# Adding the causal mask of the row maxima on VectorE inside the maximum, and making the last stage's weight parts on GpSimd alone

## The chip, the cores and the metric

The kernel runs on one core of a Trainium2 chip. The metric is the device time of one execution in microseconds (us), the median of the runs. TensorE is called PE below, VectorE DVE, ScalarE ACT, GpSimd Pool, and SP is the engine whose queue issues most DMAs. The engines run in parallel and meet only through semaphores.

## The reference, cut to what matters

Four layers follow one another on x of shape (2, 1024, 512): attention a, a feed-forward layer, attention b, the same feed-forward layer again, each behind a layer norm and with its input added. The change touches attention b, which is causal and has a linear bias per head, and the preparation of the weights of the stage behind it:

```
H, D = 32, 16
scores = jnp.einsum('bqhd,bkhd->bhqk', q, k) * SCALE
causal = rel <= 0
scores = jnp.where(causal[None, None], scores + bias[None], -jnp.inf)
attn = jax.nn.softmax(scores, axis=-1)
out = jnp.einsum('bhqk,bkhd->bqhd', attn, v).reshape(B, S, HIDDEN)
return out @ w_proj + b_proj
```

Everything is fp32. The kernel splits some operands into a high part with fewer mantissa bits and the low part that is left, and multiplies the parts.

## The kernel before, in words

The program is a chain of stages: the projections of attention a (tag pa), attention a (tag a), the stage that applies a's output projection, the feed-forward layer and b's projections (tag mid), attention b (tag b), and the last stage with b's output projection and the feed-forward layer (tag fin). Both attentions are built by one function, `attention`, and `causal` is true for b only.

**Tiling of attention.** A group is four heads of one batch element; there are 16 groups, and one step of the loop handles one group. The keys of a group lie along the free axis in row tiles: two heads (`e` = 0 and 1) sit in partitions 0 to 63 and 64 to 127 of the same tensor, so that their products use two different halves of PE's rows. A step computes each group's scores twice. The first time is for the **maxima**: a *piece* is the product of 128 queries with up to 512 keys of one head, into one of three PSUM banks (`ps_m`, `MXB = 3`), and DVE reduces it to one maximum per query (`reduce_piece`, L513). In attention b a group has 48 pieces; pieces on the diagonal are cut to 128, 256, 384 or 512 keys, and 32 of the 48 pieces are diagonal, 8 of each width. The second time is for the **scores** with keys in the partitions (`scores`, L417, into `ps_s`), where the negated maximum enters as extra rows of the product; ACT takes the exponential (L492, into `p_sb`), and `values` (L436) multiplies by the values into `ps_o`. ACT copies `ps_o` out twice a step (`copy_out`, L483), the second time at the end of the step.

**The mask.** On the diagonal the pieces and the scores both need -1e30 where the key lies after the query. `add_mask` (L355) puts it into PSUM ahead of the product: two bf16 products of a mask (64 rows by 128 columns as weights) with a half identity, 64 columns each; the product of the piece then adds to it. So each diagonal piece takes three products, and so does each diagonal score product. `mask_of_query` serves the pieces, `mask_of_key` the scores. One DMA (L333) loads the masks at the start of attention b; PE waits for it before the first piece.

**The order of the work.** PE's order is written out by hand. The pieces run 13 units ahead of the scores (`AHEAD`), which is one unit more than the 12 units of a step: the loop of step s does the scores, exponentials and values of group s and the maxima of group s + 1. Between two score products come the pieces of `ahead`. Step 15, the last, has no maxima beside it. Ahead of step 0 the first 52 pieces run with filler products between them (`keep_clock`). PE waits in `maxima` for `piece_taken` (a bank comes free), in `scores` for `exp_done` of the tile before the last, in `values` for both exponentials of the unit. DVE waits for `piece_ready`. Once a half of a group has all its maxima, DVE negates them (L519), Pool makes a high and a low part of them (`parts_of_maxima`, L266 and L269), PE turns them, DVE copies them out, and SP writes them beside the queries.

**The weights of the last stage.** `w_proj` and `w_eff` (128 x 2048 each) are needed in two parts by stage fin. Pool issues the load of `w_proj` in its loop at g = 2. ACT makes the high parts behind step 13 (`s == NG - 3`, L504), two copies in a row in ACT's own queue, ahead of the exponentials of step 14. Pool makes the low parts (L284) behind its last `parts_of_maxima`, those of group 15, and has nothing else queued until the stage ends.

Of the kernel before, what the change touches and what calls it, by code (L numbers as in the profile page):

```python
# [7 lines left out]
ALU = mybir.AluOpType  # L8
# [6 lines left out]
P = 128  # L15
# [124 lines left out]
def attention(nc, tag, causal, scale, consts, q_d, k_d, v_d, o_d, z_d, alibi_d, ones_d, first, more, output, late, to_split):  # L140
# [56 lines left out]
    with ExitStack() as ctx:  # L197
        def sb(name, shape, dt):
            return ctx.enter_context(nc.sbuf_tensor(f"{tag}_{name}", shape, dt))
# [12 lines left out]
        cparts = sb("cparts", [P, PAIR, SHIFT_ROWS, ROWS_H // PAIR], F32R)  # L212
        cturned = sb("cturned", [TURNED, P], F32)
        if causal:
            masks = sb("masks", [P, 2 * 2 * P + ROW_TILE], BF16)
            mask_of_query = masks[:, 0:2 * P].rearrange("p (a n) -> p a n", a=2)
            mask_of_key = masks[:, 2 * P:4 * P].rearrange("p (a n) -> p a n", a=2)
            half_ident = masks[:, 4 * P:]
        ps_s = ctx.enter_context(nc.psum_tensor(f"{tag}_ps_s", [P, 4, CHUNK], F32))
        ps_m = ctx.enter_context(nc.psum_tensor(f"{tag}_ps_m", [P, MXB, CHUNK], F32))  # L220
        ps_o = ctx.enter_context(nc.psum_tensor(f"{tag}_ps_o", [P, CHUNK], F32))
# [27 lines left out]
        @block.gpsimd  # L249
        def _(pool):  # L250

            pool.memset(zeros[:, :], 0.0).then_inc(zeroed, 1)
            pool.wait_ge(zeroed, 1)
            slots[1].load_k(pool, k_d, 1, alibi_d, first_loaded[0])

            def split(columns):
                return columns.rearrange("p (e n) -> p e n", e=PAIR)

            def parts_of_maxima(g, qh):

                pool.wait_ge(negated, g * 2 + (qh + 1))

                if (g, qh) != (0, 0):
                    before = turned_item(g, 0) if qh else turned_item(g - 1, 1)
                    pool.wait_ge(piece_taken, before + 1)
                pool.tensor_tensor(cparts[:, :, 0, :], split(negm[:, :]), split(zeros[:, :]),  # L266
                                   ALU.subtract).then_inc(high_ready, 1)
                pool.wait_ge(high_ready, g * 2 + (qh + 1))
                pool.tensor_tensor(cparts[:, :, 1, :], split(negm[:, :]), cparts[:, :, 0, :].bitcast(F32),  # L269
                                   ALU.subtract).then_inc(parts_ready, 1)  # L270

            parts_of_maxima(0, 0)
            slots[2].load_k(pool, k_d, 2, alibi_d, first_loaded[1])
            parts_of_maxima(0, 1)
            for g in range(1, NG):
                for qh in range(2):
                    parts_of_maxima(g, qh)
                if g == 2:
                    for to, source in late:
                        pool.dma_start(to, source).then_inc(late_loaded, 16)  # L280
            pool.wait_ge(late_loaded, 16 * len(late))
            for n, (whole, high, low_part) in enumerate(to_split):
                pool.wait_ge(w_high_ready, n + 1)
                pool.tensor_tensor(low_part[:, :, :], whole[:, :, :], high[:, :, :].bitcast(F32),  # L284
                                   ALU.subtract).then_inc(w_split, 1)
            if to_split:
                pool.wait_ge(w_split, len(to_split))
# [57 lines left out]
        def _(pe):  # L345
# [12 lines left out]
            def maxima(g, j, i):  # L358

                pair, e, qt, half, keys = pieces[i]  # L360
                if i == 0:

                    if causal and g == 0:
                        pe.wait_ge(masks_loaded, 16)
                    if j:
                        pe.wait_ge(rows_set, SETS)
                        pe.wait_ge(first_loaded[j - 1], K_LOAD)
                    wait_past(pe, qk_loaded[j], loads(g) * LOAD - (K_LOAD if j else 0))

                wait_past(pe, piece_taken, item(g, i) + (1 - MXB))  # L370
                row = ROW_TILE * e
                q = slots[j].q[row:row + crow, qt // 4, pair, qt % 4 * P:(qt % 4 + 1) * P]
                k = slots[j].k[row:row + crow, pair, half * CHUNK:half * CHUNK + keys]
                diagonal = causal and half == qt // 4
                if diagonal:
                    add_mask(ps_m[:, bank_of(g, i), keys - P:keys], mask_of_query, row)
                pe.matmul(ps_m[:, bank_of(g, i), 0:keys], q, k, start=not diagonal, stop=True,  # L377
                          skip_group_check=diagonal).then_inc(piece_ready, 1)

            def turn_maxima(g, qh):  # L380

# [95 lines left out]
        @block.scalar  # L477
        def _(act):
            def copy_out(s, qh):

                act.wait_ge(pv_done, s * NU + (last_of[qh] + 1))
                wait_past(act, out_stored[qh], s * output.STORES)
                act.activation(o_sb[:, qh, :], ps_o[:, :], ACT.Copy).then_inc(out_copied, 1)  # L483

            def step(s):
                for u, (qh, kt) in enumerate(units):
                    off = max(0, P * kt - CHUNK * qh) if causal else 0

                    wait_past(act, pv_done, s * NU + (u - 1))
                    for pair in range(2):  # L490
                        act.wait_ge(score_ready, s * NT + (2 * u + pair + 1))
                        act.activation(p_sb[:, (2 * u + pair) % NP, :, off:CHUNK],  # L492
                                       ps_s[:, 2 * pair:2 * pair + 2, off:CHUNK], ACT.Exp,
                                       scale=scale).then_inc(exp_done, 1)
                    if u == last_of[0] + 1:
                        copy_out(s, 0)
                copy_out(s, 1)

            for s in range(NG):
                step(s)  # L500
                if s == NG - 3 and to_split:
                    act.wait_ge(late_loaded, 16 * len(late))
                    for whole, high, _ in to_split:
                        act.activation(high[:, :, :], whole[:, :, :], ACT.Copy).then_inc(w_high_ready, 1)  # L504

        @block.vector
        def _(dve):
            def reduce_piece(g, i):
                pair, e, qt, half, keys = pieces[i]
                at = e * (ROWS_H // PAIR) + pair * 4 + qt % 4  # L510
                to, from_ = mxp[:, qt // 4, at, half:half + 1], ps_m[:, bank_of(g, i), 0:keys]
                dve.wait_ge(piece_ready, item(g, i) + 1)
                dve.tensor_reduce(to, from_, AX.X, ALU.max).then_inc(piece_taken, 1)  # L513

            def negated_maxima(g, qh):

                dve.wait_ge(piece_taken, item(g, (NPH, NPC)[qh] - 1) + 1)
                wait_past(dve, parts_ready, g * 2 + qh)
                dve.tensor_reduce(negm[:, :], mxp[:, qh, :, :], AX.X, ALU.max, negate=True).then_inc(negated, 1)  # L519

            def copy_turned(g, qh):
                dve.wait_ge(piece_ready, turned_item(g, qh) + 1)

                wait_past(dve, shift_loaded, g * (2 * SHIFT) + SHIFT * qh)
                dve.tensor_copy(cturned[:, :], ps_m[0:TURNED, turned_bank(g, qh), 0:P]).then_inc(piece_taken, 1)

            def ahead(s, lo, hi):

                for x in range(lo, hi):
                    past, i = divmod(x, NPC)  # L530
                    g = s + past
                    if g < NG:
                        reduce_piece(g, i)
                    if i == PPU - 1 and 0 < g <= NG:
                        copy_turned(g - 1, 1)
                    if g < NG:
                        if i == NPH + PPU - 1:
                            copy_turned(g, 0)
                        if i + 1 in (NPH, NPC):
                            negated_maxima(g, int(i + 1 == NPC))  # L540

            dve.memset(mxp[:, :, :, :], LOWEST).then_inc(filled, 1)
            dve.wait_ge(filled, 1)
            ahead(0, 0, AHEAD)
            for s in range(NG):
                ahead(s, AHEAD, AHEAD + NPC)
                if s == NG - 2:
                    output.reciprocals(dve, 0)
            output.scale(dve, 0)
# [992 lines left out]
def shape_constants():  # L1542
# [8 lines left out]
        else:  # L1551
            rot[i - DH // 2, i] = 1.0
    row, column = (np.arange(P) % ROW_TILE)[:, None], np.arange(P)[None, :]
    masks = [np.where(row + half * ROW_TILE > column, NEG, 0.0) for half in range(2)]
    masks += [np.where(column > row + half * ROW_TILE, NEG, 0.0) for half in range(2)]
    masks = np.concatenate(masks + [np.where(row == np.arange(ROW_TILE)[None, :], 1.0, 0.0)], axis=1)
    base = 2 ** (-2 ** (-(np.log2(H) - 3)))
    slopes = (base ** np.arange(1, H + 1, dtype=np.float32)).astype(np.float32)

# [35 lines left out]
```

## Time and profile before

| what | value |
|---|---|
| median of 3 runs | 1870.08 us (1851.12, 1870.08, 2012.93) |
| profiled execution, its own time | 1866.97 us |
| its span, first to last instruction | 1865.1 us, 0.2% under the median of the runs |
| mean granted TensorE clock | 0.949 of 2.4 GHz |
| PE busy over the span | 1744.0 us, 94% |
| DVE busy over the span | 1366.6 us, 73% |
| ACT busy over the span | 987.7 us, 53% |
| Pool busy over the span | 119.7 us, 6% |
| attention b, first piece to the last copy of the output | from about 1186 to 1735 us |
| last stage (fin), from that copy to the end | 130.5 us |

Times in the profile count from the start of the span. A group of instructions is given with its busy time and the mean of one in ns. Matmuls are pipelined: the busy time of one reaches from its start to the arrival of its last result, and two that run beside each other overlap, so the rate of PE is read from the distance between starts and not from busy times. The granted clock is 1.00 at 2.4 GHz and 0.50 at 1.2 GHz. "Idle before" is the time for which the engine did nothing ahead of an instruction, and the name behind the arrow is what ended it.

### The profile page before, as it was taken

How to read it: one execution, taken by the hardware profiler on the slowest of the kernel's cores; microseconds unless marked ns; L12 is line 12 of the kernel's file. 1: busy time of each engine (PE TensorE's matmuls, PEld its weight loads, DVE VectorE, ACT ScalarE, POOL GpSimd, SP SyncE). 2: the span in 40 equal slices, each digit the busy share in tenths (PEclk: the TensorE clock that was granted, in tenths of full speed). 3: DMA queues.
4: the chain of work that ended last, by engine and by line, in shares of the span. 5: the costliest groups of instructions: out<-in, count | busy, mean ns of one | idle time of the engine just before them, and what ended most of it. 6: DMA issues, size and time to landing. Idle time of an engine off the chain costs nothing. (4 is left out here: it accounts for less than half of the span.)

```text
span 1865.1 us, 35240 instructions
## 1 busy us (share of the span) xinstructions
PE 1744.0 (94%) x14412; PEld 904.9 (49%) x14412; DVE 1366.6 (73%) x2495; ACT 987.7 (53%) x1169; POOL 119.7 (6%) x218
## 2 busy tenths in 40 slices
PE   6997999999999999999799998899999999999697
PEld 4553433333333333333347677555555555543486
DVE  3765799999999999996464542588787878762485
ACT  3332277777777777778301111056666666655210
POOL 3323000000000000000010000100000000002000
PEclk9998799999999999999899999999999999975699
DMA  7768304332333333321524246815445444511221
GB/s 212 211 190 213 63 15 87 65 70 53 53 53 56 53 53 53 64 46 58 149 64 135 69 115 208 160 28 107 81 80 89 72 84 77 87 30 56 83 85 68
DMA packets 116865, 167.67 MB, mean 90 GB/s; under 512 B 20828, under 2 KB 58092, under 8 KB 116588
## 3 DMA queue, kind: packets, MB, share of 16 engines
q1 hardware_dynamic: 114880, 160.11, 38.1%
q0 software_dynamic: 1824, 5.31, 1.6%
q8 instruction: 114, 1.87, 0.4%
q14 instruction: 47, 0.39, 0.1%
HBM read 100.34 MB, written 64.50 MB: 88 GB/s over the span
## 5 line engine op out<-in xcount | busy, mean ns | idle before, releaser
L513 DVE TENSOR_REDUCE a_mxp<-a_ps_m 128x1 f32<-128x512 f32 x1024 | 634.2, 683 | 48.3 <-PE a_ps_m L377 44.9
L492 ACT ACTIVATE a_p<-a_ps_s 128x1024 f32<-128x1024 f32 x512 | 522.4, 1025 | 170.6 <-PE a_ps_s L417 160.9
L513 DVE TENSOR_REDUCE b_mxp<-b_ps_m 128x1 f32<-128x512 f32 (+3 forms) x768 | 382.3, 551 | 116.8 <-PE b_ps_m L377 109.6
L492 ACT ACTIVATE b_p<-b_ps_s 128x1024 f32<-128x1024 f32 (+3 forms) x384 | 308.8, 810 | 231.3 <-PE b_ps_s L417 229.0
L377 PE MATMUL a_ps_m<-a_slot_qk 48*128 48x512 f32 x640 | 240.0, 452 | 0.9
L417 PE MATMUL a_ps_s<-a_slot_qk 50*128 50x512 f32 x640 | 233.1, 445 | 1.2
L436 PE MATMUL a_ps_o<-a_p,a_slot_v 128*32 128x256 f32 x2560 | 205.6, 390 | 10.0 <-ACT a_p L492 5.4
L417 PEld LDWEIGHTS a_ps_s<-a_slot_qk 50*128 50x128 f32 x640 | 96.4, 185 | 128.8 <-issue 122.7
L377 PE MATMUL a_ps_m<-slot_qk 48*128 48x512 f32 x384 | 145.7, 469 | 0.4
L417 PE MATMUL a_ps_s<-slot_qk 50*128 50x512 f32 x384 | 140.3, 466 | 2.2 <-DMA slot_qk<-a_cturned 1.6
L436 PE MATMUL a_ps_o<-a_p,slot_memory 128*32 128x256 f32 x1536 | 127.9, 403 | 7.3 <-ACT a_p L492 3.3
L355 PE MATMUL b_ps_m<-b_masks 64*128 64x64 bf16 x1024 | 116.5, 197 | 2.3 <-DVE b_mxp L513 2.3
L436 PEld LDWEIGHTS a_ps_o<-a_p,a_slot_v 128*32 128x32 f32 x2560 | 54.9, 108 | 115.2 <-ACT a_p L492 101.7
L377 PE MATMUL b_ps_m<-o_qk 50*128 50x512 f32 (+3 forms) x288 | 106.3, 446 | 0.4
L355 PE MATMUL b_ps_s<-b_masks 64*128 64x64 bf16 x1024 | 102.8, 201 | 3.1 <-ACT b_p L492 3.1
L377 PEld LDWEIGHTS a_ps_m<-a_slot_qk 48*128 48x128 f32 x640 | 99.4, 185 | 9.2 <-DVE a_mxp L513 8.0
L417 PEld LDWEIGHTS a_ps_s<-slot_qk 50*128 50x128 f32 x384 | 57.6, 192 | 83.0 <-issue 76.0
L634 PE MATMUL mid_ps<-mid_q_xnt,mid_w_qkv 128*128 128x512 f32 x384 | 90.9, 398 | 5.6 <-DVE mid_q_xnt L1408 5.6
L355 PEld LDWEIGHTS b_ps_s<-b_masks 64*128 64x128 bf16 x1024 | 51.3, 97 | 90.6 <-issue 66.0
L417 PE MATMUL b_ps_s<-o_qk 52*128 52x512 f32 (+3 forms) x288 | 94.7, 453 | 0.2 <-ACT b_p L492 0.2
L417 PE MATMUL b_ps_s<-b_slot_qk 52*128 52x512 f32 (+3 forms) x240 | 86.9, 453 | 0.0
L377 PE MATMUL b_ps_m<-b_slot_qk 50*128 50x512 f32 (+2 forms) x240 | 85.8, 413 | 0.5
(166 smaller groups left out, 2453.7 us busy)
## 6 DMA issues: line engine op xcount, KB each, us to landing
va_groups<-w_o SPq DMA_DIRECT2D x16, 512.0 KB, 3.7
ka_parts<-pa_parts SPq DMA_DIRECT2D x16, 512.0 KB, 3.8
qa_parts<-pa_parts SPq DMA_DIRECT2D x32, 256.0 KB, 3.7
kb_parts<-slot_memory SPq DMA_DIRECT2D x16, 512.0 KB, 3.5
qb_parts<-slot_memory SPq DMA_DIRECT2D x32, 256.0 KB, 3.5
vb_groups<-w_proj SPq DMA_DIRECT2D x16, 512.0 KB, 3.2
a_slot_qk<-qa_parts SPq DMA_DIRECT2D x60, 128.0 KB, 4.5
a_slot_qk<-ka_parts SPq DMA_DIRECT2D x48, 128.0 KB, 6.9
```

The costliest lines, as they stand in the source:

```text
L355: pe.matmul(to[:, half * ROW_TILE:(half + 1) * ROW_TILE], mask[tile, half, :], half_ident[tile, :], start=(half == 0), stop=False, skip_gr ...
L377: pe.matmul(ps_m[:, bank_of(g, i), 0:keys], q, k, start=not diagonal, stop=True, skip_group_check=diagonal).then_inc(piece_ready, 1)
L417: mm = pe.matmul(ps_s[:, PAIR * pair + e, off:CHUNK], k, q, start=not diagonal, stop=True, skip_group_check=diagonal)
L436: mm = pe.matmul(ps_o[VW * h:VW * (h + 1), lo:hi], slots[j].v[:, kt, VW * h:VW * (h + 1)], p_sb[:, (2 * u + h // 2) % NP, h % 2, lo:hi], s ...
L492: act.activation(p_sb[:, (2 * u + pair) % NP, :, off:CHUNK], ps_s[:, 2 * pair:2 * pair + 2, off:CHUNK], ACT.Exp, scale=scale).then_inc(exp ...
L513: dve.tensor_reduce(to, from_, AX.X, ALU.max).then_inc(piece_taken, 1)
L634: mm = pe.matmul(out, lhs[a](kc), rhs[b](kc), start=(n == 0), stop=(n == len(steps) - 1))
```

## The change

The mask of the maxima is no longer put into PSUM by PE. PE issues only the product of the piece. DVE adds a mask to a diagonal piece and takes the maximum in one instruction, `tensor_tensor_reduce`: it reads the piece from PSUM and a bf16 mask from SBUF, writes the sum back into the same PSUM bank, and writes the running maximum to `mxp`. The mask for DVE is 512 columns wide, zeros and then the triangle, of which the last `keys` columns are taken; the loaded tensor grows from 576 to 832 columns. The masks of the scores stay as they are. DVE waits once for the masks' load, in group 0. The other 16 pieces of a group keep `tensor_reduce`.

The high parts of `w_proj` and `w_eff` are made by Pool, each ahead of its low part, in Pool's queue behind the last `parts_of_maxima`; the two copies on ACT are gone.

```diff
-                diagonal = causal and half == qt // 4
-                if diagonal:
-                    add_mask(ps_m[:, bank_of(g, i), keys - P:keys], mask_of_query, row)
-                pe.matmul(ps_m[:, bank_of(g, i), 0:keys], q, k, start=not diagonal, stop=True,
-                          skip_group_check=diagonal).then_inc(piece_ready, 1)
+                pe.matmul(ps_m[:, bank_of(g, i), 0:keys], q, k, start=True, stop=True).then_inc(piece_ready, 1)
...
-                dve.tensor_reduce(to, from_, AX.X, ALU.max).then_inc(piece_taken, 1)
+                if causal and half == qt // 4:
+                    if g == 0:
+                        dve.wait_ge(masks_loaded, 16)
+                    dve.tensor_tensor_reduce(from_, from_, mask_of_query[:, CHUNK - keys:], 1.0, LOWEST,
+                                             ALU.add, ALU.max, accum_out=to).then_inc(piece_taken, 1)
+                else:
+                    dve.tensor_reduce(to, from_, AX.X, ALU.max).then_inc(piece_taken, 1)
...
             for n, (whole, high, low_part) in enumerate(to_split):
+                pool.tensor_copy(high[:, :, :], whole[:, :, :]).then_inc(w_high_ready, 1)
                 pool.wait_ge(w_high_ready, n + 1)
...
-                if s == NG - 3 and to_split:
-                    act.wait_ge(late_loaded, 16 * len(late))
-                    for whole, high, _ in to_split:
-                        act.activation(high[:, :, :], whole[:, :, :], ACT.Copy).then_inc(w_high_ready, 1)
```

## Rows read from the trace of the kernel before

**Rows 1.** The page, part 2: PE busy and granted clock in 40 slices of the span.
```profile
PE   6997999999999999999799998899999999999697
...
PEclk9998799999999999999899999999999999975699
```

**Rows 2.** Busy time by stretch: steps 1 to 13, step 14, step 15, the last stage.
```profile
core 0: us, PE busy (x) PEld busy (x) DVE busy (x) ACT busy (x) POOL busy (x), PEclk, DMA share, GB/s
1247.36:1648.05 400.69, 397.17 (x5050) 214.60 (x5046) 319.74 (x676) 263.65 (x339) 12.09 (x53) 1.00 0.48 84
1648.05:1698.82 50.77, 48.13 (x382) 23.37 (x378) 26.31 (x50) 23.86 (x29) 6.15 (x6) 0.55 0.04 10
1698.82:1734.62 35.80, 34.25 (x272) 12.42 (x268) 2.50 (x4) 20.11 (x26) 3.69 (x1) 0.50 0.25 72
1734.62:1865.10 130.48, 104.71 (x448) 84.98 (x448) 87.14 (x162) 17.96 (x33) 4.06 (x4) 0.88 0.25 84
```

**Rows 3.** Timeline of ACT around the end of step 13: start, us, engine, line.
```profile
1648.05 0.60 ACT L483 ACTIVATE out_b_sums<-b_ps_o 128x512 f32<-128x512 f32 x1 [0.63 <-PE b_ps_o L436]
1648.54 1.90 ACT L504 ACTIVATE w_proj_high<-w_proj 128x2048 fp32r<-128x2048 f32 x1
1650.34 1.90 ACT L504 ACTIVATE w_eff_high<-w_eff 128x2048 fp32r<-128x2048 f32 x1
1652.14 1.93 ACT L492 ACTIVATE b_p<-b_ps_s 128x1024 f32<-128x1024 f32 x2
```

**Rows 4.** Timeline of PE behind them.
```profile
1653.21 0.23 PE L355 MATMUL b_ps_s<-b_masks 64*128 64x64 bf16 x1 [2.64 <-ACT b_p L492]
```

**Rows 5.** Busy time in short stretches on either side of a change of the clock.
```profile
1195.50:1198.90 3.40, 3.08 (x18) 1.45 (x17) 2.46 (x6) 0.00 (x0) 3.24 (x8) 1.00 1.07 154
205.70:209.10 3.40, 1.83 (x8) 0.88 (x8) 2.19 (x4) 0.00 (x0) 0.00 (x0) 1.00 0.46 58
209.10:212.50 3.40, 3.40 (x16) 1.91 (x18) 3.03 (x6) 2.21 (x3) 0.00 (x0) 0.50 0.00 0
...
1649.50:1652.90 3.40, 1.07 (x13) 0.75 (x12) 1.63 (x5) 3.40 (x3) 0.00 (x0) 1.00 0.22 48
1652.90:1656.30 3.40, 3.09 (x32) 1.76 (x32) 0.89 (x3) 1.98 (x3) 0.00 (x0) 0.51 0.15 41
```

**Rows 6.** Timeline of PE in step 7: a diagonal piece with its two masks.
```profile
1443.14 0.23 PE L355 MATMUL b_ps_m<-b_masks 64*128 64x64 bf16 x2
1443.21 0.36 PE L377 MATMUL b_ps_m<-b_slot_qk 50*128 50x256 f32 x1
```

**Rows 7.** Waits between 1220 and 1640: us in total, times, longest.
```profile
DVE b_mxp L513 <- PE b_ps_m L377: 76.6, 137, 1.4
...
PEld b_ps_m L355 <- DVE b_mxp L513: 14.2, 43, 0.5
...
PEld b_ps_m L377 <- DVE b_mxp L513: 7.6, 28, 0.3
```

**Rows 8.** Groups of DVE's instructions by shape, between 1220 and 1640: busy us, mean ns.
```profile
L513 DVE TENSOR_REDUCE b_mxp<-b_ps_m 128x1 f32<-128x512 f32 x330 | 209.6, 683 | 33.2 <-PE b_ps_m L377 31.9
...
L513 DVE TENSOR_REDUCE b_mxp<-b_ps_m 128x1 f32<-128x128 f32 x108 | 26.0, 281 | 2.3 <-PE b_ps_m L377 2.3
```

**Rows 9.** Groups of DVE over the whole span: other forms that take two tensors, and a small one.
```profile
L1391 DVE SCALAR_TENSOR_TENSOR slot_memory<-mid_ps,b_qk,slot_memory 128x512 fp32r<-128x512 f32 x32 | 23.5, 749 | 45.7 <-ACT slot_memory L1331 45.7
...
L1379 DVE TENSOR_TENSOR x_sb<-mid_ps,x_sb 128x512 f32<-128x512 f32 x32 | 21.1, 686 | 36.4 <-PE mid_ps L1284 36.4
...
L519 DVE TENSOR_REDUCE b_negm<-b_mxp 128x16 f32<-128x32 f32 x32 | 5.9, 186 | 1.1
```

**Rows 10.** Timeline of Pool in steps 14 and 15.
```profile
1693.32 0.22 POOL L269 TENSOR_TENSOR b_cparts<-b_negm,b_cparts 128x16 fp32r<-128x16 f32 x1
1693.50 4.52 POOL L284 TENSOR_TENSOR w_proj_low<-w_proj,w_proj_high 128x2048 fp32r<-128x2048 f32 x1
1697.97 4.54 POOL L284 TENSOR_TENSOR w_eff_low<-w_eff,w_eff_high 128x2048 fp32r<-128x2048 f32 x1
```

**Rows 11.** Group of Pool: the nearest row to a plain write of 128 x 2048.
```profile
L983 POOL MEMSET w_o<- 128x2048 f32 x1 | 1.8, 1804 | 0.3 <-POOLq L1584 0.3
```

More of the change, by code:

```diff
@@ L214, in attention @@
         if causal:
[L215 to L218, printed above, removed]
+            masks = sb("masks", [P, 2 * P + ROW_TILE + CHUNK], BF16)
+            mask_of_key = masks[:, 0:2 * P].rearrange("p (a n) -> p a n", a=2)
+            half_ident = masks[:, 2 * P:2 * P + ROW_TILE]
+            mask_of_query = masks[:, 2 * P + ROW_TILE:]
         ps_s = ctx.enter_context(nc.psum_tensor(f"{tag}_ps_s", [P, 4, CHUNK], F32))
@@ L1553, in shape_constants @@
     row, column = (np.arange(P) % ROW_TILE)[:, None], np.arange(P)[None, :]
-    masks = [np.where(row + half * ROW_TILE > column, NEG, 0.0) for half in range(2)]
-    masks += [np.where(column > row + half * ROW_TILE, NEG, 0.0) for half in range(2)]
-    masks = np.concatenate(masks + [np.where(row == np.arange(ROW_TILE)[None, :], 1.0, 0.0)], axis=1)
+    masks = [np.where(column > row + half * ROW_TILE, NEG, 0.0) for half in range(2)]
+    masks += [np.where(row == np.arange(ROW_TILE)[None, :], 1.0, 0.0), np.zeros((P, CHUNK - P))]
+    masks += [np.where(column > np.arange(P)[:, None], NEG, 0.0)]
+    masks = np.concatenate(masks, axis=1)
     base = 2 ** (-2 ** (-(np.log2(H) - 3)))
```

## The prediction

> **What bounds the kernel now.** I read the page first, for the clock by slices [rows 1]: PE is busy nearly everywhere, and its clock falls under 0.9 in few slices, most of all in the three from about 1632 us on, which are the end of attention b and the start of the last stage. Then I cut attention b by steps, from one end-of-step copy on ACT to the next [rows 2]. Steps 1 to 13 take 400.69 us, 30.82 us each, all at clock 1.00. PE is busy for 99% of them by the page's way of counting, DVE for 24.6 us a step (319.74 / 13, 80%), ACT for 20.3 us (66%). Step 14 has the same work, takes 50.77 us, and its clock is 0.55. Step 15, without maxima, takes 35.80 us at 0.50.
>
> The reason for step 14 stands in the timelines. At the end of step 13 ACT makes the two high parts, from 1648.54 to 1652.24, before the first exponential of step 14 [rows 3]; PE runs out of free score banks and idles for 2.64 us until 1653.21 [rows 4]. In the short stretch around this gap PE is busy for 1.07 of 3.40 us, and behind it the clock is 0.5, that is 1.2 instead of 2.4 GHz [rows 5]. The same had happened at 209 us: 1.83 busy of 3.40, and the next stretch is at 0.50. With 3.08 of 3.40 the clock stayed at 1.00 [rows 5]. It stays low to the end of attention b: 48.13 us of step 14 without the gap against 30.82.
>
> **Part 1, the copies leave ACT.** Step 14 loses the gap and keeps the clock: 50.77 - 30.82 = 19.95 us saved. Step 15 at the full clock is on no row. Scaled as step 14 is (30.82 / 48.13 = 0.64) it takes 22.9 us; ACT alone is busy for 20.1 of it [rows 2] and becomes a larger share, so I take 24 us, a saving of 11.8. The bounds are 20.1 (ACT without a pause, 15.7 saved) and 35.8 (the clock is lost again before it, nothing saved). The last stage behind it is left at its 130.48 us; it begins with a chain of stores and loads while PE idles, so its clock starts low either way.
>
> **Part 2, Pool takes them.** Pool's queue is empty behind the last parts of the maxima. There the two low parts run now, 4.52 and 4.54 us [rows 10]. No row shows a Pool copy of 128 x 2048: the bounds are a fill, 1.80 us [rows 11], and the subtraction that reads two inputs, 4.52. With 4.5 (it reads and writes, nearest to the subtraction) the chain is 18.1 us. It begins some 5.5 us before the end of step 14 in the slow clock (1693.32 against 1698.82) and about 3.5 us before it in the fast one, so it ends 14.6 us into step 15. The cover is the rest of step 15, 24 us long: 9 us are left. DVE has 2.5 us of work in step 15 [rows 2], so nothing disturbs it. Cost: 0. Were the cover gone, the end of the stage would be late by what sticks out, at most a few us.
>
> **Part 3, PE loses the masks of the maxima.** 32 pieces a step lose two small products and their two weight loads. The product of the piece starts 0.07 us after the first mask [rows 6]; all on the path this would be 2.24 us a step, but the two halves of the rows (`e` = 0 and 1) work side by side, so 1.12 at most, and 0 where the other half, DVE or ACT sets the pace. I take 0.5 us a step: PE paces the step, since its own waits for DVE are 21.8 us in 420 [rows 7], but much of the time it is the other row half, with score masks that stay, that ends last.
>
> **Part 4, DVE does more.** The reduction takes 683 ns for 512 keys and 281 for 128 [rows 8]: 1.05 ns a column over about 147. The new form is on no row. The adding form with one input in PSUM takes 686 ns, the form with scalar and two tensors 749 [rows 9]. Lower bound: +3 ns, as the addition; I allow nothing below it, since each element must still be read once at the same rate. Upper bound for a form at that rate: +186 ns, when the running maximum is written by a second small instruction that costs what the smallest reduction does [rows 9]. I take +66 ns, the row nearest in kind (scalars, two tensors, fixed work). That is 2.1 us more DVE time a step (32 x 0.066) in 6.2 us of idle time, most of it waiting for PE [rows 7]. It delays PE only where the three banks are full, 71 times in 420 us [rows 7], some 5 a step: 0.25 us a step, between 0 and 2.1.
>
> The Trainium skill (VectorE: DVE Perf Modes, "Two Vector instructions with no wait between them") says that an instruction which also writes out its accumulator is two instructions, the main one and a read of the accumulator. No row here has such a pair. By it the second instruction would be there; the sum with it is that of the rival on DVE below.
>
> Ahead of step 0, 36 diagonal pieces get the slower form: at most 36 x 0.066 = 2.4 us, and PE, slowed by fillers, gives 0 to 2.5 back; I count 0. The wider mask load and DVE's one wait for it cost nothing: PE waits for the same load before the first piece.
>
> **Sum.** 1866.97 - 19.95 - 11.8 - 15 x (0.5 - 0.25) = 1831.5 us against the profiled execution. That execution was 0.2% under the median of 1870.08, so against the median the same savings give 1834.6. I forecast 1833, 2.0% faster. What a measurement can tell from no change here is about 2%, so the likeliest case lies on that border.
>
> **Rivals.**
> *The clock is lost again (0.20).* Without maxima step 15 leaves PE waiting for ACT, and a pause there, above all at the small units of the diagonal, may do what the gaps at 205.7 and 1649.5 did [rows 5]. Lost at the start of step 15: +11.8, 1845; lost in the middle of step 14 as well, another 9: 1854. For it: once low the clock stayed low for the whole end of the stage. Against it: 467 us at 1.00 before the gap, which hold 13 equal steps. The fastest of the three runs, 1851, may be an execution of this kind.
>
> *DVE becomes a bound (0.14).* With +186 ns a piece DVE needs 24.6 + 6.0 = 30.6 us of a 30.8 us step, and the idle time left between bursts is no longer there: some 2 us a step and 6.7 us ahead of step 0 (36 x 0.186). 1833 + 15 x 2 + 5 = 1868. Against it: every form with one operation per element on the rows is within 66 ns of the reduction.
>
> *The new form runs at half the rate (0.05), the one that ends slower.* It reads and writes PSUM and reads SBUF in one instruction; if that costs a second pass per column, a mean diagonal piece of 320 columns takes 0.335 us more, DVE 35.3 us a step, 4.5 over the present step, and 12 us more ahead of step 0. 1833 + 15 x 4.5 + 12 = 1912. It is slower than before from about 0.19 us a piece on, where DVE is full, and by over 2% from about 0.34 us on.
>
> *Fewer products let the clock fall inside the steps (0.04).* 64 of some 388 products a step are gone (5050 in 13 steps [rows 2]). A step at 0.50 costs 17.3 us more (48.13 against 30.82); five such steps eat the gain and another two bring 1920. Against it: the masks are 64 columns each, little of PE's real work.
>
> *The change doesn't do what it says (0.03).* If Pool's chain reached past the end of attention b or into the start of the last stage, some of part 1 would come back: 9 us too late, 1842.
>
> The forecast has 0.54: its own range is 1820 (step 15 at 20.1 us, masks worth 1.1 us a step) to 1850 (step 15 half at the low clock, DVE's delay 1 us a step). The range to hold 8 in 10 reaches from 1815 to 1868, with the clock and most of the DVE case in it. Faster by over 2% means under 1832.7: somewhat over half of the forecast case and little else, 0.34. Slower by over 2% are the half rate and the clock falling inside the steps: 0.09. The rest, 0.57, is within 2%.
>
> **What would show it.** Step 14 at 30.5 us with clock 1.00 and no row of L504 on ACT shows part 1; step 15 at about 24 us its second half. Steps 1 to 13 at 30.5 to 30.7 us show parts 3 and 4; the mean of the new DVE form at 512 keys (near 750 ns), or a second row beside it, shows which value of part 4 holds. Pool's four instructions should end before step 15 does. The forecast is wrong if the clock falls at another place than 1652.9, or if DVE's busy time comes near that of the step.

## The result and the profile after: 12% slower, with the clock at half

The changed kernel takes 2090.05 us (2081.2, 2088.09, 2102.07, 2092.01), against 1866.21 for the kernel before, median of four: 1.123 times as long [1.113, 1.134]. The prediction was 1833 (1815 to 1868), with 0.09 on slower. The ratios here and below leave out runs more than 1.5% above the fastest of their kernel; for before these are the 2012.93 us and, in a later series, 2009.84 us at a mean clock of 0.860 (the profiled run had 0.949), of which no trace was kept, so it isn't shown that the kernel before always holds the clock. The profiled execution after took 2081.2 us, its span is 2079.4 us.

The page's part 2 of the kernel after, PE busy and granted clock in 40 slices, answers to [rows 1]:

```profile
PE   6997999999999999979999999999999999999798
...
PEclk9999899999999999989999965556555565556789
```

PE is busier than before, and its clock is near 0.5 from the twenty-fourth slice on, 1.2 GHz where it had been 2.4. Before, only the last slices of attention b looked so. The cut by steps, as in [rows 2], says where. Its rows: the time up to the end of step 0 from the first maxima, steps 1 to 13, step 14, step 15, the last stage; then, from other answers of the same view, the stretches on either side of two falls of the clock. Columns as in [rows 2].

```profile
1174.06:1259.60 85.54, 84.05 (x444) 40.18 (x444) 54.62 (x177) 19.93 (x26) 9.87 (x25) 0.70 0.31 57
1259.60:1876.40 616.80, 616.15 (x4216) 293.19 (x4214) 354.31 (x1092) 266.31 (x339) 12.11 (x53) 0.52 0.32 54
1876.40:1917.90 41.50, 41.37 (x326) 19.61 (x324) 26.53 (x78) 20.44 (x26) 3.12 (x6) 0.62 0.05 12
1917.90:1948.80 30.90, 28.61 (x272) 10.41 (x271) 3.14 (x5) 19.90 (x26) 10.50 (x3) 0.67 0.29 83
1948.80:2079.40 130.60, 104.12 (x448) 84.47 (x448) 87.14 (x162) 17.96 (x33) 4.06 (x4) 0.89 0.26 84
...
1211.60:1215.00 3.40, 3.20 (x27) 2.06 (x26) 2.87 (x12) 1.94 (x2) 0.00 (x0) 1.00 0.05 10
1215.00:1218.40 3.40, 3.40 (x29) 1.40 (x26) 2.17 (x10) 1.53 (x3) 0.00 (x0) 0.50 0.00 0
...
1447.10:1450.50 3.40, 3.21 (x29) 2.08 (x26) 2.83 (x12) 2.51 (x3) 0.00 (x0) 1.00 0.16 34
1450.50:1453.90 3.40, 3.40 (x29) 1.45 (x26) 2.16 (x10) 1.51 (x3) 0.00 (x0) 0.51 0.39 95
```

Against [rows 2] the span grows by 214.3 us: 12.2 up to the end of step 0, 216.1 in steps 1 to 13, then -9.3 in step 14, -4.9 in step 15 and +0.1 in the last stage. The clock falls at 1215.0, inside step 0, stays at 0.50 for 221.9 us, is back for 13.65, falls again at 1450.5, and so on: 1686.1 and 1921.6. A step wholly at 0.50 takes 48.57 us; the full clock comes back for the last 10.3 us of a step, which takes 41.95, and the first 3.3 us of the next, which takes 47.9. There is no gap of the length of [rows 5] ahead of a fall: PE is busy for 3.20 of 3.40 us, more than the 3.08 of a stretch in which the clock of before held at 1.00, and far from the 1.07 that came before the fall at 1652.9 [rows 5].

Is it DVE's new form that paces the steps? Groups of DVE's instructions by shape, after, between 1220 and 1640 (line, operation, count, busy us, mean ns, idle before), to be read beside [rows 8]:

```profile
L512 DVE TENSOR_REDUCE b_mxp<-b_ps_m 128x1 f32<-128x512 f32 x144 | 93.5, 686 | 55.8 <-PE b_ps_m L375 55.8
L509 DVE CUSTOM_DVE_ANT_0 b_ps_m<-b_ps_m,b_masks 128x512 f32<-128x512 f32 x70 | 47.3, 714 | 17.9 <-PE b_ps_m L375 17.9
L509 DVE DVE_READ_ACCUMULATOR2_ANT b_mxp<- 128x1 f32 x278 | 39.1, 141 | 0.0
L509 DVE CUSTOM_DVE_ANT_0 b_ps_m<-b_ps_m,b_masks 128x384 f32<-128x384 f32 x68 | 37.9, 572 | 46.1 <-PE b_ps_m L375 46.0
L509 DVE CUSTOM_DVE_ANT_0 b_ps_m<-b_ps_m,b_masks 128x256 f32<-128x256 f32 x70 | 29.7, 437 | 34.1 <-PE b_ps_m L375 34.0
L509 DVE CUSTOM_DVE_ANT_0 b_ps_m<-b_ps_m,b_masks 128x128 f32<-128x128 f32 x70 | 19.8, 308 | 23.9 <-PE b_ps_m L375 23.9
```

It isn't. Every group of pieces idles for PE (L375 is the piece's product), 178 us in 420, where before it was 77 [rows 7]. DVE is busy for 354.31 us of 616.80. What one instruction costs is 31 ns more at 512 columns, and there is a second instruction behind it, which the last section comes back to. So time is lost on PE alone, by its clock, and the experiments ask what took the clock.

### The profile page after: what moved, and what is told of

Read it like the earlier page. It is cut to its first block and busy times, and to the rows that moved or that the text cites. A ratio compares the mean times of both kernels' runs of the same rounds, so it can differ in the third digit from the quotient of the medians.

```text
span 2079.4 us, 33734 instructions
## 1 busy us (share of the span) xinstructions
PE 1964.1 (94%) x13388; PEld 980.4 (47%) x13388; DVE 1406.5 (68%) x3007; ACT 987.0 (47%) x1167; POOL 123.5 (6%) x220
## 5 line engine op out<-in xcount | busy, mean ns | idle before, releaser
L509 DVE CUSTOM_DVE_ANT_0 b_ps_m<-b_ps_m,b_masks 128x128 f32<-128x128 f32 (+3 forms) x512 | 245.2, 509 | 208.5 <-PE b_ps_m L375 207.7
L375 PE MATMUL a_ps_m<-a_slot_qk 48*128 48x512 f32 x640 | 239.1, 451 | 0.9
L512 DVE TENSOR_REDUCE b_mxp<-b_ps_m 128x1 f32<-128x512 f32 x256 | 166.1, 686 | 93.3 <-PE b_ps_m L375 93.3
L375 PE MATMUL a_ps_m<-slot_qk 48*128 48x512 f32 x384 | 145.2, 468 | 0.5
L375 PE MATMUL b_ps_m<-o_qk 50*128 50x512 f32 (+3 forms) x288 | 135.5, 566 | 0.4 <-DVE b_mxp L509 0.2
L414 PE MATMUL b_ps_s<-o_qk 52*128 52x512 f32 (+3 forms) x288 | 132.5, 616 | 0.2 <-ACT b_p L489 0.2
L356 PE MATMUL b_ps_s<-b_masks 64*128 64x64 bf16 x1024 | 128.5, 236 | 0.8 <-ACT b_p L489 0.8
L375 PE MATMUL b_ps_m<-slot_qk 50*128 50x512 f32 (+2 forms) x240 | 122.5, 593 | 0.3 <-DVE b_mxp L509 0.2
L375 PE MATMUL b_ps_m<-b_slot_qk 50*128 50x512 f32 (+2 forms) x240 | 122.4, 592 | 0.3 <-DVE b_mxp L509 0.2
L414 PE MATMUL b_ps_s<-slot_qk 52*128 52x512 f32 (+3 forms) x240 | 119.4, 628 | 0.0
L414 PE MATMUL b_ps_s<-b_slot_qk 52*128 52x512 f32 (+3 forms) x240 | 119.0, 628 | 0.0
L433 PE MATMUL b_ps_o<-b_p,v_memory 128*32 128x256 f32 (+1 forms) x960 | 112.2, 562 | 1.3 <-ACT out_b_sums L480 0.7
```

Of the source, the lines that this page charges most:

```text
L356: pe.matmul(to[:, half * ROW_TILE:(half + 1) * ROW_TILE], mask[tile, half, :], half_ident[tile, :], start=(half == 0), stop=False, skip_gr ...
L375: pe.matmul(ps_m[:, bank_of(g, i), 0:keys], q, k, start=True, stop=True).then_inc(piece_ready, 1)
L414: mm = pe.matmul(ps_s[:, PAIR * pair + e, off:CHUNK], k, q, start=not diagonal, stop=True, skip_group_check=diagonal)
L433: mm = pe.matmul(ps_o[VW * h:VW * (h + 1), lo:hi], slots[j].v[:, kt, VW * h:VW * (h + 1)], p_sb[:, (2 * u + h // 2) % NP, h % 2, lo:hi], s ...
L509: dve.tensor_tensor_reduce(from_, from_, mask_of_query[:, CHUNK - keys:], 1.0, LOWEST, ALU.add, ALU.max, accum_out=to).then_inc(piece_take ...
```

## The experiments

A *step* below is the distance between two end-of-step copies on ACT; before it is 30.82 us (steps 1 to 13), 50.77 (14) and 35.80 (15). Times are medians of all runs of a kernel; where its two runs differ by much, both are given. "Low" and "full" clock are the granted 0.50 and 1.00.

### One part alone: the weight parts on Pool (e1_pool_only, again as e8_pool_only_3)

```diff
             for n, (whole, high, low_part) in enumerate(to_split):
+                pool.tensor_copy(high[:, :, :], whole[:, :, :]).then_inc(w_high_ready, 1)
...
-                if s == NG - 3 and to_split:
-                    ... (ACT's two copies)
```

> The kernel before with the second half of the change alone: Pool makes the high parts, ACT's two copies are gone, the masks stay on PE. Theory A (the products of the masks keep the clock up; without them it falls in the steps): the clock stays at 1.00 through step 14, step 14 takes 30.8 us instead of 50.8, step 15 between 23 and 36; total 1833 to 1848 us. Theory B (moving the copies to Pool is part of the slowdown): over 1900 us, with clock 0.50 in the steps.

> The kernel before with Pool making the high parts, again, in three rounds for an interval: 1825 to 1835 us, 0.975 to 0.985 of before by theory A; the candidate for the fastest version.

1828.62 us, 0.982 [0.974, 0.990]; as e8 1831.41, 0.982 [0.975, 0.989]. Steps 1 to 13, step 14 and step 15 of e1, busy time by stretch:

```profile
1243.87:1644.48 400.61, 397.14 (x5050) 214.51 (x5046) 319.73 (x676) 263.63 (x338) 12.09 (x53) 1.00 0.49 84
1644.48:1674.85 30.37, 30.09 (x382) 15.96 (x378) 24.60 (x50) 20.29 (x26) 3.27 (x6) 1.00 0.07 16
1674.85:1698.90 24.05, 20.67 (x272) 8.44 (x268) 3.12 (x5) 19.84 (x27) 10.36 (x3) 1.00 0.33 107
```

The clock is 1.00 to the end of attention b. This half of the change is the whole gain, 32 us, and no part of the loss.

### The other part alone: no masks of the maxima on PE (e2_pe_masks_gone), and its control (e9_zero_bias)

The piece's product stands alone, DVE keeps the plain reduction, ACT keeps its copies. Both kernels have a bias table of zeros, so that the maxima without a mask stay in range; e9 is the kernel before with that table and nothing else.

```diff
-                diagonal = causal and half == qt // 4
-                if diagonal:
-                    add_mask(ps_m[:, bank_of(g, i), keys - P:keys], mask_of_query, row)
-                pe.matmul(..., start=not diagonal, ...)
+                pe.matmul(ps_m[:, bank_of(g, i), 0:keys], q, k, start=True, stop=True).then_inc(piece_ready, 1)
...
+    ramp = 0 * ramp
```

> The kernel before without the 1024 mask products of the maxima on PE; DVE keeps its plain reduction and ACT its two copies. Left out of the computation: the mask in the maxima, and the linear bias of attention b (its table is zero). Theory A (fewer products alone let the clock fall): most steps of attention b at 0.50, 45 to 49 us each, total 2050 to 2100 us. Theory C (DVE's longer instruction pair, by making PE wait, is what lets the clock fall): steps 0 to 13 at 1.00 and 30.3 us, total 1855 to 1865 us.

> The kernel before with the table of the linear bias set to zero and nothing else changed: the control for the runs that left the bias out. Left out: the linear bias of attention b. If the data play no part: as before, 1850 to 1870 us, steps of 30.8 us, the first fall in attention b at about 1650 us. If the zeros themselves let the clock fall: over 1950 us, and the runs without mask products say nothing.

e2: 2101.11 us, 1.128 [1.114, 1.142]. Stretches of e2 on either side of the fall, and steps 1 to 13:

```profile
1218.00:1222.80 4.80, 4.65 (x35) 2.77 (x38) 4.00 (x11) 2.17 (x3) 0.04 (x1) 1.00 0.02 5
1222.80:1227.60 4.80, 4.80 (x46) 2.47 (x38) 2.60 (x5) 2.08 (x3) 0.00 (x0) 0.50 0.00 0
1266.35:1894.00 627.65, 627.65 (x4216) 300.67 (x4214) 337.40 (x676) 266.23 (x339) 12.07 (x53) 0.50 0.32 53
```

With DVE's form and Pool's part out of the kernel the loss is all there. The clock falls at 1222.8 and stays low for 768 us, past the end of attention b; PE is busy for every one of the 627.65 us of steps 1 to 13. e9 was 1863.34 us in its profiled run, with steps of 30.8 and the first fall at 1652.1, as the kernel before. Its other run took 1958.47 us at a mean clock of 0.893 (0.954 in the profiled one), without a trace. So the zeros don't need to cost the clock, but by e9 alone it isn't shown that they play no part. What carries e2 is its comparison with e12 below, which has the same zeros and holds the clock in both runs.

### Half of the masks kept (e7_half_the_masks)

As e2, but one head of each pair keeps its masks on PE.

```diff
-                diagonal = causal and half == qt // 4
+                diagonal = causal and half == qt // 4 and e == 1
```

> The kernel before with the mask products of the maxima on PE for one of the two heads of a pair alone, 512 instead of 1024; ACT keeps its copies. Left out of the computation: half of the mask of the maxima, and the linear bias (its table is zero). Theory A: somewhere between before (no fall ahead of 1652 us) and none (cold from 1222 us on): either cold stretches in some steps, 1900 to 2000 us, or cold in all, 2080; no effect (1860) would mean that the mask's second half of the rows is what counts.

2118.48 us, 1.137 [1.128, 1.146]: slower than with none, at 49.49 us a step, the clock low for 764.6 us from 1209.2 on. That is outside the 1900 to 2080 us expected: half of the masks kept nothing of the clock. The stretch ahead of the fall:

```profile
1204.40:1209.20 4.80, 4.78 (x41) 3.00 (x40) 3.91 (x12) 1.70 (x2) 0.43 (x2) 1.00 0.02 5
```

PE is busy for 4.78 of 4.80 us and the clock falls all the same.

### DVE's form alone (e3_dve_form_only)

PE keeps its masks, ACT its copies; DVE adds its mask as well on diagonal pieces, from a 512-column mask of its own.

```diff
-                dve.tensor_reduce(to, from_, AX.X, ALU.max).then_inc(piece_taken, 1)
+                if causal and half == qt // 4:
+                    ...
+                    dve.tensor_tensor_reduce(from_, from_, wide_mask[:, CHUNK - keys:], 1.0, LOWEST,
+                                             ALU.add, ALU.max, accum_out=to).then_inc(piece_taken, 1)
+                else:
+                    dve.tensor_reduce(to, from_, AX.X, ALU.max).then_inc(piece_taken, 1)
```

> The kernel before with DVE's new form on the diagonal pieces alone; the mask products stay on PE too (the mask is added twice) and ACT keeps its two copies. Theory A (fewer products are the cause): clock 1.00 in steps 0 to 13, each about 0.3 us longer than 30.82; total 1865 to 1880 us. Theory C (DVE's form is the cause): the clock falls early in attention b and the total is over 2050 us.

1893.58 us, 1.017 [1.010, 1.024]. Three steps of e3 at the full clock and the one behind them:

```profile
1241.49:1334.96 93.47, 92.64 (x1170) 50.16 (x1166) 78.24 (x252) 60.81 (x79) 3.40 (x13) 1.00 0.52 92
1334.96:1381.01 46.05, 46.03 (x394) 22.82 (x390) 27.41 (x84) 20.50 (x26) 0.88 (x4) 0.59 0.34 54
```

The stretches ahead of its two falls in steps 1 to 13:

```profile
1335.90:1339.30 3.40, 3.39 (x42) 2.02 (x41) 3.34 (x16) 2.48 (x3) 0.00 (x0) 1.00 0.19 41
1506.50:1509.90 3.40, 3.39 (x37) 1.93 (x36) 3.37 (x16) 2.42 (x3) 0.00 (x0) 1.00 0.19 41
```

A step at the full clock takes 93.47 / 3 = 31.16 us, 0.34 more than before. Twice, at 1339.3 and 1509.9, the clock falls for 37.5 us, with PE busy for 3.39 of the 3.40 us ahead, and a step takes 46.06; that is 2 x 14.9 = 29.8 us of the 34.2 by which these thirteen steps are longer than before (434.87 against 400.69). The expectation had neither the falls nor 1894 us. So DVE's form alone is enough to lose the clock now and then; that its later answer is what does it is argued and not shown.

### The change with PE's masks back (e4_change_with_pe_masks)

e1 and e3 together, which is the change with this restored:

```diff
+                if diagonal:
+                    add_mask(ps_m[:, bank_of(g, i), keys - P:keys], mask_of_query, row)
```

> The changed kernel with the mask products of the maxima put back on PE (the mask is added twice): DVE's new form and Pool's parts as in the change. Theory A: the clock stays up and the step takes about 31.1 us, total 1835 to 1855 us. Theory C: as slow as the changed kernel, over 2050 us.

2045.68 us and 1963.0. Three steps of 31.17, then falls at 1339.8 and 1380.8, the second for 542.7 us, with steps of 50.23. The masks alone don't restore the clock where DVE has the longer form. That was a miss: with e3 at 1894 and e1 at 1829 the sum of both would be near 1860. The two kernels, e3 and e4, differ only in who makes the weight parts, and nothing of that runs before the end of step 13. Up to there the clock of both falls first at 1339.3 and 1339.8, and then again, for 37.5 us in e3 and for the rest of step 13 and beyond in e4. So how long a fall lasts isn't fixed by the instructions: the 150 us between e3 and e4 stand in thirteen steps that both run alike (434.87 and 586.65 us), and aren't the price of an edit.

### Work put in their place (e5, e6, e13, e10)

All have the change's DVE form and Pool's part. e5_four_small_fillers issues the two mask products twice per diagonal piece; e6_wide_filler puts one bf16 product of 256 columns, whose result is overwritten, ahead of each diagonal piece, and no mask; e13_narrow_filler one of 128 columns; e10_wide_filler_one_head that of 256 for `e == 1` only.

```diff
+                diagonal = causal and half == qt // 4
+                if diagonal:                                  # e10: and e == 1
+                    tile = slice(row, row + ROW_TILE)
+                    pe.matmul(ps_m[:, bank_of(g, i), 0:2 * P], mask_of_key[tile, 0, :], masks[tile, 0:2 * P],
+                              start=True, stop=True)          # e13: 0:P
                 pe.matmul(ps_m[:, bank_of(g, i), 0:keys], q, k, start=True, stop=True).then_inc(piece_ready, 1)
```

> The changed kernel with four mask products instead of none ahead of each diagonal piece on PE (the piece then overwrites or adds to them; the mask stays right). Theory A (it is the amount of PE's work in the steps that keeps the clock): the clock stays at 1.00 in nearly all steps, a step takes about 31.6 us, total 1845 to 1870 us. Theory D (something of the new DVE form lets the clock fall whatever PE does): again cold stretches of tens to hundreds of us, over 1900 us.

> The changed kernel with one bf16 product of 256 columns in place of the two masks' 64 + 64 columns ahead of each diagonal piece; the piece overwrites it. Twice the columns of the masks, half the products and half the weight loads. If columns streamed are what keeps the clock: 1.00 in nearly all steps, 1840 to 1870 us. If it is the number of products or weight loads: cold steps as in the run with two masks or worse, over 1930 us.

> The changed kernel with one bf16 product of 128 columns ahead of each diagonal piece, 32 a step: the columns per step of the two masks and of the run with 16 products of 256, one product and one weight load instead of two. If the sum of columns decided alone, it would behave as both, which behaved differently, so one of them must be matched: clock falls and 1900 to 2050 us if it is the length of a product or its place that counts; clock held, steps of 30.7 us and 1830 to 1845 us if the small products of 64 columns with their loads are what is worth little.

> The changed kernel with the product of 256 columns ahead of the diagonal pieces of one head of each pair alone, 16 a step instead of 32: as many columns per step as the mask products had. If the sum of columns decides, this is near the edge: the clock falls now and then, 1850 to 2050 us, as with the two masks back on PE (2004). If it holds: steps of 30.6 us and 1830 to 1845 us.

| kernel | us | ratio to before | step, 1 to 13 | clock in attention b |
|---|---|---|---|---|
| e5 | 1859.49 | 0.998 [0.994, 1.001] | 32.13 (31.8 in most) | two falls of 3.4 us |
| e6 | 1839.88 | 0.987 [0.979, 0.995] | 30.85 | first fall at 1692.3 |
| e13 | 1842.21 | 0.988 [0.984, 0.993] | 30.84 | first fall at 1689.5 |
| e10 | 1840.2 | 0.986 [0.983, 0.990] | 30.72 | first fall at 1676.4 |

e10, steps 1 to 13, step 14 and step 15:

```profile
1243.46:1642.78 399.32, 393.20 (x4425) 203.87 (x4422) 338.27 (x1092) 263.98 (x338) 12.21 (x53) 1.00 0.49 84
1642.78:1673.10 30.32, 29.85 (x340) 15.24 (x337) 25.85 (x78) 20.31 (x27) 3.16 (x6) 1.00 0.07 17
1673.10:1707.98 34.88, 32.72 (x272) 11.80 (x268) 3.10 (x5) 19.96 (x27) 10.46 (x3) 0.55 0.23 74
```

Sixteen products a step whose results nobody reads take the changed kernel from 2090 to 1840 us. Work for PE was what the change took away. Two of e5's eight runs took 1974.77 and 1882.33 us, at mean clocks of 0.891 and 0.948 (0.974 in its trace), so it doesn't always hold the clock; e6, e13 and e10 have two runs each, within 0.6% of one another. Step 15, which has no maxima and so no filler, loses the clock in e6, e13 and e10 (34.88 us in e10 against the 24.05 of e1), but not in e5 (24.04).

### The filler without DVE's form (e12_wide_filler_plain_reduce)

e6 with the plain reduction, zero bias, and neither mask: it is e2 with the filler and with Pool's part.

```diff
-                    dve.tensor_tensor_reduce(...)
+                dve.tensor_reduce(to, from_, AX.X, ALU.max).then_inc(piece_taken, 1)
...
+    ramp = 0 * ramp
```

> As the changed kernel with the product of 256 columns ahead of each diagonal piece, but DVE keeps its plain reduction: against that run this gives the cost of DVE's new form at the full clock. Left out: the mask in the maxima and the linear bias. The clock holds, steps of 30.5 to 30.8 us against 30.85, total 1825 to 1838 us; if DVE's form cost nothing, the steps are equal.

1833.5 us, 0.983 [0.979, 0.986]. Steps 1 to 13:

```profile
1239.45:1635.73 396.28, 391.69 (x4633) 207.84 (x4630) 319.72 (x676) 263.88 (x338) 12.18 (x53) 1.00 0.49 85
```

30.48 us a step at 1.00, where e2 has 48.28 at 0.50. This is the cleanest pair: the same step with 32 products more is 17.8 us shorter. Against e6 it prices DVE's form at 30.85 - 30.48 = 0.37 us a step.

### Is it only the passage into step 0? (e11_wide_filler_first_groups)

The filler of e6 for groups 0 and 1 only. From step 1 on every step is the change's own.

```diff
-                if diagonal:
+                if diagonal and g <= 1:
```

> The changed kernel with the product of 256 columns ahead of the diagonal pieces of groups 0 and 1 alone. Theory A (each step needs the work): step 0 at 1.00, then the clock falls within a step or two and most later steps take 48 us, total 2020 to 2090 us. Theory E (only the passage from the first maxima into step 0 is critical, later steps hold by themselves): steps of 30.6 us throughout, 1830 to 1860 us.

1952.14 and 2088.87 us. Profiled: steps 1 to 7, step 8, steps 9 to 14, step 15:

```profile
1244.04:1457.75 213.71, 209.18 (x2272) 107.81 (x2270) 182.00 (x588) 142.19 (x182) 6.93 (x29) 1.00 0.51 87
1457.75:1505.95 48.20, 48.01 (x328) 22.34 (x326) 27.33 (x84) 20.50 (x26) 0.88 (x4) 0.53 0.31 51
1505.95:1789.43 283.48, 283.14 (x1946) 134.37 (x1944) 163.66 (x498) 123.01 (x156) 10.40 (x26) 0.52 0.27 46
1789.43:1821.76 32.33, 30.62 (x272) 11.17 (x269) 2.50 (x4) 20.07 (x26) 7.59 (x3) 0.60 0.28 80
```

Seven steps of the change run at 1.00, 213.71 / 7 = 30.53 us each. In the eighth, which has the same instructions, the clock falls. The fall was expected within a step or two, and came after seven; the other run, 2088.87 us at a mean clock of 0.810, is as slow as the changed kernel. So the start of attention b isn't special: the change's step can run at either clock, and it doesn't hold the full one for long.

### The filler to the end (e14_filled_to_the_end)

e10, with the same product also ahead of each off-diagonal score product of step 15.

```diff
+                if causal and s == NG - 1 and not diagonal:
+                    tile = slice(row, row + ROW_TILE)
+                    pe.matmul(ps_s[:, PAIR * pair + e, 0:2 * P], mask_of_key[tile, 0, :], masks[tile, 0:2 * P],
+                              start=True, stop=True)
```

> The changed kernel with a product of 256 columns ahead of the diagonal pieces of one head of each pair, and one ahead of each score product off the diagonal in step 15. Steps of 30.7 us with the clock at 1.00 to the end of step 15, which takes 24 to 26 us instead of 34.9: 1826 to 1834 us, level with the kernel before whose weight parts alone were moved to Pool (1831). Should the fillers delay ACT in step 15: up to 1840 us.

1831.41 us, 0.985 [0.980, 0.990], four runs. Step 15 takes 28.38 us (24 to 26 expected), with a fall of 13.7 us at 1671.2. It equals e8 (1831.41) and doesn't beat it. The version to keep is thus the kernel before with Pool's part alone: 32 us below before, and simpler than any with a filler.

## Why the prediction was wrong, step by step

**Part 1, the copies leave ACT: right.** Alone it gave step 14 30.37 us (30.82 forecast) and step 15 24.05 (24 forecast).

**Part 2, Pool's chain is hidden: right in effect, wrong in size.** Timeline of Pool in the kernel after, beside [rows 10]:

```profile
1915.52 1.89 POOL L283 CAST w_proj_high<-w_proj 128x2048 fp32r<-128x2048 f32 x1
1917.49 4.54 POOL L285 TENSOR_TENSOR w_proj_low<-w_proj,w_proj_high 128x2048 fp32r<-128x2048 f32 x1
1921.97 1.89 POOL L283 CAST w_eff_high<-w_eff 128x2048 fp32r<-128x2048 f32 x1
1923.94 4.53 POOL L285 TENSOR_TENSOR w_eff_low<-w_eff,w_eff_high 128x2048 fp32r<-128x2048 f32 x1
```

A copy takes 1.89 us, not 4.5: the fill of [rows 11], 1.80, was the near row, and I took the subtraction. The chain is 13 us and ends at 1928.5, 20 us before step 15 does.

**Part 3, PE without the masks: right at the full clock.** e11's steps against e3's: 30.53 - 31.16 = -0.63 us (-0.5 forecast).

**Part 4, DVE's form: right at the full clock.** +0.34 us a step (e3 against before) and +0.37 (e6 against e12), where +0.25 stood. The net of both parts is e11's 30.53 against a forecast of 30.57. Timeline of DVE after, two diagonal pieces in a row:

```profile
1206.04 0.56 DVE L509 CUSTOM_DVE_ANT_0 b_ps_m<-b_ps_m,b_masks 128x384 f32<-128x384 f32 x1
1206.51 0.14 DVE L509 DVE_READ_ACCUMULATOR2_ANT b_mxp<- 128x1 f32 x1
1206.51 0.60 DVE L509 CUSTOM_DVE_ANT_0 b_ps_m<-b_ps_m,b_masks 128x384 f32<-128x384 f32 x1
1207.03 0.14 DVE L509 DVE_READ_ACCUMULATOR2_ANT b_mxp<- 128x1 f32 x1
```

The second instruction is there, as the Trainium skill says (VectorE: DVE Perf Modes, "Two Vector instructions with no wait between them"); it overlaps the next main one, so that the 141 ns are not added. Read from starts where DVE doesn't wait, at 512 columns: behind a plain reduction of before the next instruction starts most often 598 or 608 ns later, behind the new form in e6, at the full clock, 606 or 649 ns. That is 51 ns more at the most, under the +66 taken and far from +186. The rival on DVE and that of the half rate are dead by these rows.

**The sum: right for a clock that holds, and it didn't hold.** The step that failed is the rival "Fewer products let the clock fall inside the steps", which had 0.04. Its price was right: 17.3 us a step forecast, 48.57 - 30.53 = 18.0 measured. Its sum was not: at 17.3 us a step two such steps eat the gain, not five, and five in all bring 1920; the trace has steps 1 to 13 low nearly throughout, and they cost 216 us. What was wrong is the argument that gave it so little, "the masks are 64 columns each, little of PE's real work". e2 shows that removing just these products takes the clock, e12 that other idle products give it back, and e13 and e10 that few suffice, with the change's own DVE form and the true bias. I had looked for a pause, since a pause stood ahead of both falls of [rows 5], and asked only whether the change adds one. It adds none of that length (3.20 us busy of 3.40). I had also read the 467 us at 1.00 as a margin. They show that the old step held in that execution, not by how much; e3, with the same products and the new form on DVE, falls twice in them.

The Trainium skill (TensorE: Matmul & The Clock Gate, "A second HAM failure mode: psum-queue depth-cycling") tells of a kernel whose PE pauses briefly and often between groups of products while it cycles through PSUM banks, and whose clock goes back and forth. It is nearer to this case than the gap I looked for, and I didn't weigh it. The maxima cycle through three banks here and in the changed kernel the clock falls four times; the trace differs in that it stays low for 222 us at a stretch, with PE busy for 616.15 of 616.80 us.

**Shown and not shown.** Shown: without the mask products on PE the clock is lost though DVE keeps its plain form (e2 against e12, which differ in the steps by the fillers alone); DVE's form alone loses the clock at times (e3); otherwise idle PE work restores it in the changed kernel (e6, e10, e13). Open: which property of PE's work decides. The page's busy share doesn't tell: 99% in e3's steps, which fell (92.64 of 93.47), 99% in those of before, which held (397.17 of 400.69), and 98.5% in e10's, which held. Nor does the count of products: 390 in a step of e3 (1170 / 3), 340 in one of e10 (4425 / 13). e4 with 64 small products in a step fell where e10 with 16 and e13 with 32 larger ones held. Open too is how often each kernel loses the clock, before included: e4 and e11 have two runs 80 us or more apart, and runs of before, e5, e8 (1877.95 us) and e9 had mean clocks of 0.860 to 0.948, with no trace to say where it was low. "Holds" and "falls" are thus read from one trace of each kernel and the times of few runs. A way to put work on PE without taking its time wasn't tried.

## What to carry to other kernels

On an engine whose clock follows its activity, products that look like overhead may be what keeps the clock: before taking small ones off, ask what the step costs at the low clock (here 18 us for a hoped 0.5) and give that case a real chance, even where the trace shows hundreds of us at full clock. When such a change comes out slow, read the granted clock by stretch first, and put idle products where the old ones were: one run tells lost clock from lost time. Then look at more than one run: over the same thirteen steps the clock was low for 75 us in one trace and for 475 in another (e3, e4). Split a change with two parts: here one was worth 32 us and the other cost 259 (2090 against 1831).

## What the hardware showed that I had not expected

- The clock fell from 1.00 to 0.50 with PE busy for 4.78 of 4.80 us (e7). It stayed there for 222 us of work without a pause in the changed kernel (PE busy for 221.80 us of the 221.80 from 1215.0 on), for 765 and 768 us in e7 and e2, and for only 37.5 us in e3. The first falls of after lie 235.5 and 235.6 us apart.
- The same instructions ran at either clock in one execution (e11): 30.53 and 48.57 us a step. In e3 and e4 the same instructions in steps 1 to 13 fell at nearly the same moment (1339.3 and 1339.8) and then stayed low for very different times.
- DVE's combined form is an instruction of 714 ns at 128x512 and a read of 141 ns, and yet what follows starts at most 51 ns later than behind the reduction (649 against 598).
- Pool copies 128x2048 from fp32 to fp32r in 1.89 us and subtracts in 4.54.
